# A four-layer graph network on one core: the index columns of the first gather are made ahead of the tile counting

## The reference

```python
src = jax.random.randint(..., (100000,), 0, 6250, jnp.int32)
dst = jax.random.randint(..., (100000,), 0, 6250, jnp.int32)
_o = jnp.argsort(dst, stable=True)
src = src[_o]
dst = dst[_o]
...
# layer 0
h = _bn(x @ w1.T + b1, g1, beta1)
agg = jax.ops.segment_sum(h[src], dst, num_segments=n)
conv = agg @ wr.T + br + h @ wroot.T
out = _bn(gelu(conv) @ w2.T + b2, g2, beta2) + x
# layer 1: by src, from dst, weighted
gathered = support[edge_col] * edge_val[:, None]
out = jax.ops.segment_sum(gathered, edge_row, num_segments=x.shape[0])
# layer 2: three graph convolutions; layer 3: messages with edge features
...
x = _layernorm(x + layer(x), axis=-1)     # after each layer
```

## Time and profile before

| | us |
|---|---|
| median of 3 timed runs (7656.18 to 7658.34) | 7657.89 |
| the profiled execution, its own time | 7638.33 |
| its span, first to last instruction | 7636.6 |
| POOL busy | 5467.9 (72%) |
| PE busy | 4281.3 (56%) |
| DVE busy | 2093.6 (27%) |
| ACT busy | 477.9 (6%) |
| share of POOL in the chain that ended last | 51% |

### The profile page before, as it was taken

The page is one execution under the profiler, slowest core; times in us unless marked ns, Lnnn a source line. Parts: engine busy times, 40 slices in busy tenths (PEclk is TensorE's granted clock), DMA queues, the critical chain, the costliest instruction groups (busy, mean ns, idle before and its releaser), DMA issues.

```text
span 7636.6 us, 57592 instructions
## 1 busy us (share of the span) xinstructions
PE 4281.3 (56%) x14386; PEld 3081.9 (40%) x14386; DVE 2093.6 (27%) x4076; ACT 477.9 (6%) x1351; POOL 5467.9 (72%) x5587
## 2 busy tenths in 40 slices
PE   4655558810046556455656755557655556555557
PEld 2433347710034444333444544445444434443436
DVE  6344412500022222411111211112111114444445
ACT  0000002200000000000000200002000001000002
POOL 5777777777767777377777577775777774777774
PEclk9776778955577777778777877878777777777678
DMA  2333331000023333333333333333333334666661
GB/s 73 103 88 90 91 103 43 19 18 1 1 72 105 105 105 105 95 103 103 104 104 104 105 104 105 104 105 104 110 104 104 105 104 124 194 197 195 196 197 62
DMA packets 423702, 774.25 MB, mean 101 GB/s; under 512 B 121791, under 2 KB 273269, under 8 KB 423413
## 3 DMA queue, kind: packets, MB, share of 16 engines
q0 software_dynamic: 250240, 616.54, 28.2%
q1 hardware_dynamic: 173172, 154.00, 6.3%
HBM read 730.40 MB, written 39.71 MB: 101 GB/s over the span
## 4 chain that ended last, share of the span: by engine, by line
POOL 51%; issue 19%; PE 17%; DMA 8%; DVE 5%; SPq 0%; ACT 0%; DVEq 0%; POOLq 0%; ACTq 0%
POOL ring L404 41%; PE acc L546 13%; POOL records_by_src L420 10%; DMA ring<-table_g,idx_dst 4%; PE acc L471 2%; DVE onehot L991 2%; DMA ring<-in_x_dram,idx_dst 1%; DMA ring<-table_x,idx_dst 1%; DVE H L904 1%; DMA ring<-table_y,E 1%; DVE X L1023 1%; PE acc L466 1%; DVE ring L1004 1%; PE bank L457 1%; DVE ring L1005 0%
## 5 line engine op out<-in xcount | busy, mean ns | idle before, releaser
L546 PE MATMUL acc<-ring,onehot 128*128 x9984 | 3599.6, 524 | 2582.5 <-SPq L219 1727.2
L546 PEld LDWEIGHTS acc<-ring,onehot 128*128 128x128 f32 x9984 | 2485.9, 260 | 3692.0 <-issue 3234.9
L404 POOL DMA_INDIRECT ring<-table_g,idx_dst x2346 | 2250.7, 959 | 932.8 <-issue 653.0
L994 DVE TENSOR_TENSOR onehot<-iota_row,dl_dst 128x512 f32<-128x512 f32 x1040 | 721.1, 694 | 3170.6 <-PE acc L546 3169.9
L404 POOL DMA_INDIRECT ring<-in_x_dram,idx_dst x782 | 835.1, 1068 | 302.3 <-issue 219.0
L404 POOL DMA_INDIRECT ring<-table_x,idx_dst x782 | 809.3, 1035 | 326.8 <-issue 316.8
L404 POOL DMA_INDIRECT ring<-table_y,E x782 | 743.5, 951 | 274.6 <-issue 221.8
L420 POOL DMA_INDIRECT records_by_src<-E x782 | 752.7, 963 | 238.4 <-issue 238.4
L991 DVE TENSOR_SCALAR onehot<-iota_row,E 128x128 f32<-128x128 f32 x832 | 235.4, 361 | 777.5 <-PE acc L546 777.3
L1004 DVE TENSOR_TENSOR ring<-ring,E 128x1024 f32<-128x1024 f32 x196 | 239.9, 1224 | 547.8 <-DMA ring<-table_x,idx_dst 547.5
L515 PE MATMUL bank<-ident,E 128*128 128x128 f32 (+1 forms) x7 | 1.7, 402 | 592.2 <-ACT E L830 592.2
(11 more groups left out here) (265 smaller groups left out, 2214.8 us busy)
## 6 DMA issues: line engine op xcount, KB each, us to landing
E<-in_edge_attr_dram SPq DMA_DIRECT2D x781, 128.0 KB, 3.1
ring<-table_g,idx_dst POOLq DMA_INDIRECT x2346, 2.7
table_g<-H SPq DMA_DIRECT2D x147, 128.0 KB, 1.7
ring<-in_x_dram,idx_dst POOLq DMA_INDIRECT x782, 2.8
records_by_src<-E POOLq DMA_INDIRECT x782, 2.1
ring<-table_y,E POOLq DMA_INDIRECT x782, 2.7
ring<-table_x,idx_dst POOLq DMA_INDIRECT x782, 3.5
table_y<-ring SPq DMA_DIRECT2D x49, 128.0 KB, 2.0
```

The costliest lines, as they stand in the source:

```text
L404: pool.indirect_dma_start(out=ring_v[:, b % SLOTS, 0:D], out_offset=None, in_=table[name][:, :], in_offset=bass.IndirectOffsetOnAxis(ap=id ...
L546: pe.matmul(acc4[:, ds(to, width)], onehot[:, (q * BATCH + j) % ONEHOTS, :], ring[:, ds(slot, width)], start=False, stop=True, skip_group_ ...
L994: last = tt(onehot[:, s:s + BATCH, :], iota_row[:, :].unsqueeze(1).to_broadcast((P, BATCH, P)), dl_ap[which][:, q * BATCH:(q + 1) * BATCH] ...
```

## The change

The turning of the edge sources is written ahead of everything else on PE, and its input is made by ACT as soon as the loads of the sources are in (`src_in`) and no longer after `edges_ready`. POOL's gather waits for `edges_ready` besides `idx_ready`. ACT makes `srcf` a second time after `edges_ready`, for the unsorted case, and DVE waits for that (`src_kept`) before it works on `srcf` at q = 1. In the branch for unsorted edges SP loads `idx_dst` by 25 DMAs from the ordered records; it is not entered here.

```diff
@@ -240,7 +240,13 @@
-                sp.wait_ge(sm("taken_back"), 16 * KT * 3)
+                    sp.wait_ge(sm("idx_ready"), 1)
+                    for b in range(0, B, 32):
+                        n = min(32, B - b)
+                        sp.dma_start(idx["dst"][:, b:b + n],
+                                     rec_u_dram[b * P:(b + n) * P, 1:2].rearrange("(b e) w -> e (b w)", e=P))\
+                          .then_inc(sm("taken_back"), 16)
+                sp.wait_ge(sm("taken_back"), 16 * (KT * 3 + -(-B // 32)))
             sp.sem_inc(sm("edges_ready"), 1)
@@ -411,6 +417,7 @@
             pool.wait_ge(sm("idx_ready"), 1)
+            pool.wait_ge(sm("edges_ready"), 1)
             gather(0)
@@ -546,13 +553,14 @@
+            pe.wait_ge(sm("constants"), 1)
+            pe.wait_ge(sm("turnable"), 1)
+            turn_edges(srcf, (4, 5)).then_inc(sm("idx_turned"), 1)
             pe.wait_ge(sm("constants"), 2)
             pe.wait_ge(sm("disorder_counted"), 1)
             one(bank[7][:, 0:1], ones[:, :], dcol[:, :]).then_inc(sm("disorder_mm"), 1)
             tile_starts(0, "dst")
             tile_pairs(0, "dst")
-            pe.wait_ge(sm("turnable"), 1)
-            turn_edges(srcf, (4, 5)).then_inc(sm("idx_turned"), 1)
             pe.wait_ge(sm("idx_ready"), 1)
@@ -782,9 +790,11 @@
-            act.wait_ge(sm("edges_ready"), 1)
+            act.wait_ge(sm("src_in"), 96)
             sc.copy(srcf, src_i).then_inc(sm("turnable"), 1)
             keep_idx("dst", 1)
+            act.wait_ge(sm("edges_ready"), 1)
+            sc.copy(srcf, src_i).then_inc(sm("src_kept"), 1)
             act.wait_ge(sm("tables_done"), 1)
@@ -1081,6 +1091,7 @@
                 if q == 1:
+                    dve.wait_ge(sm("src_kept"), 1)
                     link(tt(key_s, key_s, mask, ALU.max))
```

## The result

Over 11 timed runs each, the changed kernel takes 7631.89 us in the median (7625.07 to 7646.45), the kernel before 7653.78 (7650.98 to 7658.46). The ratio is 0.9974, 95% interval 0.9967 to 0.9982: 20 us less by the ratio, 21.9 by the medians. The forecast was 19.3 less and a median of 7638.6 within 7634 to 7652. Most of that is in the starting value of the sum, as worked out further down.

The account below looks back on a forecast made before the run. Up to 2135 us everything hangs on POOL's gathers; the 65th moves from 150.24 to 130.56 + 0.4 = 131.0, 19.3 earlier. So 7638.3 - 19.3 = 7619.0 profiled, plus 19.6 gives a median of 7638.6, range 7634 to 7652.

Parts of the forecast that it names:

- the starting value of the sum: Whole kernel: profiled execution 7638.3 us before, timed runs 19.6 above it before and after, so the median starts from 7657.9.
- The step that carried it: Aggregation 0: 64 ring slots fill by 96 us, POOL stops, and PE's batches 0 to 12 release the 65th gather at 131.0.
- First gather: Front, POOL: starts at about 14.4 to 14.8 us, after index columns and `edges_ready`, some 54 us earlier than before.
- The delay of the counting: Front, DVE: waits for the disorder product, queued behind PE's transposes; 0.4 us late, bounds 0 and 1.2.
- PE's pace: Aggregation 0, PE's batches up to 12: 2.19 us apart at full clock, without idling; batch 12 ends at 130.27.
- POOL's wake-up: Ring wait in aggregation 0: 0.29 us from the signal to POOL's gather.
- The 65th gather of the kernel before: Aggregation 0, POOL: taken to start at 150.24 us, so starting at 131.0 makes it 19.3 us earlier.
- Everything behind it moves by the same: After the 65th gather: the rest of aggregation 0, the records and what waits for them move by the same 19.3 us.
- (a): POOL's head start: the ring does not hold it and all 54 us come through, 7604 us; chance 0.02.
- (b): Front: POOL's gathers get nowhere while DVE counts, a gain of 6, 7652 us; chance 0.04.
- (c): Front: gathers hold up DVE's 49 counts, adding 47 us, net 27 slower, 7685 us; chance 0.03.
- (d): Later stages or a late start signal: over 4 us of the gain lost, 7643 to 7655, taken as 7648; chance 0.13.

Follow-up runs that it names:

- late start: Changed kernel with POOL's first gather also waiting for the end of DVE's counts: ratio 0.9994 to the kernel before.
- the kernel with both changes: Changed kernel with 23 of 49 counts moved to ACT and the tighter ring wait of aggregation 0: 7605.38 us, ratio 0.9927 to the kernel before.
- half of the counts: Changed kernel with 23 of the 49 counts on ACT and the disorder product ahead of the transposes: 7613.65 us, ratio 0.9937 to the kernel before.
- tight ring: Changed kernel, aggregation 0's ring wait asking only what evenly spread edges need, not the worst case of 49 tiles: 7621.21 us, ratio 0.9946 to the kernel before.
- e_lock: Changed kernel with a float32 copy of the keys after each of DVE's counts: ratio 1.0012 to the kernel before.

## Why the prediction was right, and where it was not

**The step that carried it** held: the head start counts only until the ring is full, and PE sets the restart. Forecast 131.0 for the 65th gather, measured 131.03 and 131.83. Its parts:

- *First gather* at 14.4 to 14.8: it was 20.34. The columns and `edges_ready` were there by about 15 (ACT's second cast, released by the same signal, started at 15.03); the 5 us behind that are put down to no other engine ("issue"). They hang on the disorder: in the six traces with the early start on the first kind of chip the first gather comes 6.4 to 6.6 us after the end of DVE's cast of the disorder (13.84 to 20.34 here). POOL reads the disorder there and passes over the branch for unsorted edges, some 1300 rows of its program; in the kernel before and in the late start, which did that long before their signal, the first gather follows the signal within 0.3 and 1.0 us (68.67 to 68.96, and 64.56 after the counts' last result at 63.5). Which part of the reading and the passing over takes the 5 us was not tried. The prediction left this term out, without a reason. It cost nothing, as POOL stood 27.6 us later; in the kernel with both changes, where POOL never stands, it costs its 5 us.
- *The delay of the counting*, taken as 0.4 within 0 to 1.2: 1.06. ACT's cast of the sources started at 10.26 where 9.5 was taken. How much of it reaches PE's first batch a single pair of traces can't tell: 102.29 against 101.84 in the first, but PE's table products alone take 12.16 to 13.52 us from trace to trace, and with the same front the first batch is at 101.85 in the late start and at 103.05 in the changed kernel's second trace.
- *PE's pace* in the four batches without a row, 2.19 at a clock of 1.00: 2.2 at 1.00. PE did not idle, and the clock stayed up, as forecast.
- *POOL's wake-up* 0.29: 0.27.
- *The 65th gather of the kernel before* was the wrong row; the term is 20.5 and not 19.3.
- *PE's batch k - 3 must be done for batch k*: by the wait in the code it is batch k - 4, as 53 for k = 16 stands for batches 0 to 12. The forecast used the right one there.

**Everything behind it moves by the same**: shown by the four kernels on one chip. Lead and gain of the total by the medians (7664.93 before): late start 3.1 and 4.7; changed 19.7 and 20.8; half of the counts 44.2 and 51.3; tight ring 45.6 and 43.7. One for one, within 1 to 7 us; the leads are of single traces, with the kernel before on another chip.

**The rivals.** (a), the full 54 us, fell with the ring; the kernel with both changes shows that 50 are to be had without it. (b) and (c) did not come true for the counts, whose lengths and the gathers' beside them stayed, though e_lock shows that (b) needed only another instruction. On the slower chips something like (c) does happen. (d), a loss later on, looked true in the first pair of traces (23.7 at the first record, 6.6 at the end) and was the spread of single executions.

**The step that failed** is the last one of the sum, its starting value: "The timed runs lie 19.6 above it, which is as much the case before as after, so the median goes from 7657.9". Three things were wrong in it.

- *The median of the kernel before* came from three runs, 7657.89; eleven give 7653.78, and on two later occasions it was 7660.0 and 7664.9. That is 4.1 of the 6.7 us by which the forecast missed.
- *The spread*, "some 2 us" in the range, was read from those three. Eleven runs of the kernel before spread over 7.5 us, those of the changed kernel over 21. Even by its own terms the lower end is 7635 (7637 less 2) and not 7634.
- *The 19.6* is no offset common to both kernels. The profiled execution of the changed kernel took 7631.76, 0.1 from its median and not 19.6 below it, and 12.8 above the 7619.0 that the prediction gave for it; the second one of the kernel before took 7669.40, above its median. The 7638.33 lies 11 us below the shortest of 61 other executions of the kernel before on chips of the first kind (7649.20); why it was so short stays open.

The gain was too small by the 1.25 us of the wrong row. With 4.1 less in the base and 1.25 more in the gain the same sum gives 7633.2; the last 1.3 us lie within the spread. So the mechanism held and the base was mis-sized. On the occasion with 7664.9 before, the changed kernel had 7644.16, 5.5 above the forecast and inside the range: with medians that move by 11 us from occasion to occasion, on which side of 7634 the result falls is partly chance. As for the chances, most was put on faster by over 0.2%: the ratio is 0.26% below one, but its interval, 0.18 to 0.33%, reaches a little under 0.2.

## What to carry to other kernels

A head start into a buffer of fixed depth is worth the consumer's restart, not the producer's: find the wait behind the last free slot, and work out when the consumer satisfies it. Then look at what that wait asks for; here a worst-case margin of 49 in a wait on a count cost another 23 us, and work ahead of the consumer that an idle engine could share cost 30. Read the spread from executions on more than one occasion before a range is drawn, and never the end of a single pair of traces: a lead of 23.7 us early on showed as 6.6 at the end and as 37 in another pair.

## What the runs showed of the hardware

**Two kinds of chip.** On chips A and B the same program takes 17% longer. Windows from 1250 to 1400 us, while POOL writes records (busy of PE, PEld, DVE, ACT, POOL, clock, DMA share, GB/s), first of the changed kernel on a chip of the first kind, then on A:

```profile
1250.00:1400.00 150.00, 146.25 (x1311) 146.05 (x1310) 34.52 (x135) 44.43 (x131) 113.97 (x119) 1.00 0.03 3
```

```profile
1250.00:1400.00 150.00, 26.53 (x56) 17.60 (x56) 4.93 (x7) 0.87 (x4) 113.95 (x119) 0.51 0.02 1
```

POOL's pace is the same, 119 instructions. On the first chip the three others are at dense products; on A they are still summing aggregation 0, with all its blocks gathered, and manage 7 batches in 150 us, with DVE idle for most of the time and no releaser named ("remote"). In the counting on A, DVE's counts start to stand apart 36 us after POOL's first gather:

```profile
55.43 1.09 DVE L914 TENSOR_SCALAR_CACHE_REDUCE H<-H 128x896 f32<-128x896 f32 x1
57.53 1.09 DVE L914 TENSOR_SCALAR_CACHE_REDUCE H<-H 128x896 f32<-128x896 f32 x1 [1.01 <-issue]
61.03 1.09 DVE L914 TENSOR_SCALAR_CACHE_REDUCE H<-H 128x896 f32<-128x896 f32 x1 [2.40 <-remote]
```

The counts themselves take 1.09 as ever. With the late start, whose first gather is at 64.55, the counts run through to their end, and DVE's gaps begin at 88.3, in the tables; the longest is this:

```profile
133.67 1.08 DVE L988 SCALAR_TENSOR_TENSOR dl_dst<-X,bank 128x416 f32<-128x416 f32 x2 [31.32 <-remote]
```

PE's first batch is at 155.30 in place of 101.85. And where POOL stands at the ring wait of the changed kernel on A (100 to 165 us), PE's batches come every 2.2 us as on the other chips. So the gaps move with POOL's stream of indirect DMAs and end with it: on these chips that stream holds the other engines between their instructions. Why these chips and not the others, and by what path, is open; no run tried it.

**Kinds of DVE instructions differ in what they do to POOL.** Beside counts with a running sum an indirect DMA takes 0.946 us in the median, in step with float32 copies 1.36, beside a scan 1.76.

**ACT counts as fast as DVE.** Sign with a sum over 128x896 takes 1034 ns, DVE's comparison with a sum 1080.
